# Recommender tower, one core: early chunks in another order, weight preparation between them, gathers issued without waits

## The chip, the core and the metric

The kernel runs on one NeuronCore of a Trainium2 chip. The core has five engines that work in parallel, each through its own instructions in order: TensorE (PE, matrix products; its weight loads are shown as PEld), VectorE (DVE), ScalarE (ACT), GpSimd (POOL) and SyncE (SP, which here only issues DMA transfers). Engines are held together by semaphores: an instruction waits until a counter has reached a value. The metric is the device time of one execution in microseconds. SBUF is the working memory on the core, PSUM the memory that TensorE writes.

## What is computed

A recommendation tower for 512 samples. 26 rows of 64 numbers are gathered for each sample from 26 tables (13,312 rows in all); they are projected, normalised over 128 features, mixed to 32 rows for each sample, normalised over these 32, and multiplied pairwise with each other and with a normalised dense row. The 528 products go through a linear layer and a norm, and then through a small network with the dense inputs beside them:

```python
x = layer_norm(dense_t @ Wd.T, gd, bd)
y = layer_norm(jnp.einsum('bnd,ed->bne', sparse_t, Ws), gs, bs)
y = jnp.einsum('bne,pn->bep', y, Wsi)
y = layer_norm(y, gsi, bsi)
y = jnp.swapaxes(y, 1, 2)
T = jnp.concatenate([x[:, None, :], y], axis=1)
Z = jnp.einsum('bnd,bmd->bnm', T, T)
Zflat = Z[:, TRIL_I, TRIL_J]
out = layer_norm(Zflat @ Wl.T, gl, bl)
...
h = jnp.concatenate([z, r_dense_t], axis=1)
h = jnp.maximum(h @ W_top1 + b_top1, 0.0)
h = jnp.maximum(h @ W_top2 + b_top2, 0.0)
y = h @ W_top3
```

Of the linear layer's 512 columns the network uses the first 384. All arithmetic is in float32.

## The kernel before

The 512 samples are cut into 4 groups of 128 (`NG`), and each group into 4 chunks of 32 (`NC`); chunk n is chunk n % 4 of group n // 4, and there are 16. In the texts c stands for n % 4. POOL gathers the embedding rows with 104 indirect DMAs (L332), 26 for a group, in batches of 8, 6, 6 and 6 for its chunks. The waits ahead of them (`steps`, from chunk 2 on) tie each gather of chunk n to a step of VectorE or TensorE in chunk n - 2; the memory that a gather writes is used by it alone, so no data hangs on these waits.

A chunk n passes through these steps, each a function of the engine's program:

- `transpose_rows` (PE, L1039) turns its gathered rows, ACT copies them from PSUM (`gt_copy`, L424), and `gram_rows` (PE, L1045) multiplies them by a Gram matrix, from which VectorE gets the first variance (`variance1`, L748 and L752). ACT takes its root (`deviation1`, L429) and VectorE scales the rows (`scale_rows`, L766).
- `project_fields` (PE, L1057) mixes the 26 rows to 32, ACT copies the result (`ut_copy`, L433: the projected rows' copy), and `embed` (PE, L1070) applies the projection.
- `y_evacuate` (DVE, L780) adds a bias and writes the chunk into V; `square2` (ACT, L438), `variance2` (DVE, L787), `deviation2` (ACT, L442: the second root) and `normalise2` (DVE, L794 and L796) are the second norm.
- `pair_products` (PE, L1077) forms the products, `z_evacuate` (ACT, L448 to L450) and `z_merge` (DVE, L838) take them to SBUF.

A group, once its four chunks are merged, goes through `spread_pairs` (PE, L1165), `z_copy` (ACT, L499), `project_pairs` (PE, L1119, five blocks of 128), `f_squares` and `deviation3` (ACT), `root3` (DVE), `f_scale` (ACT), `transpose_features` (PE), `zn_copy` (ACT) and `layer1`, `layer2`, `layer3` (PE, L1135, L1145, L1153) with their copies.

The order of the work is written out by hand: each engine runs a function `slot(n)`, for n = 3 to 14 (2 to 14 on VectorE), between a written-out beginning and a written-out end. A slot mixes steps of chunks n, n - 1, n - 2 and n - 3 with steps of the group before. PE's slot is: transpose n, project n - 1, Gram of n, embed n - 1, pair products of n - 2, with one piece of group work in each slot.

Weights are prepared on the chip as well, once: `prepare_b1` (PE, L1001) multiplies 12 blocks of the first layer's weights by a single column each, which is 24 passes of TensorE; `prepare_dense` (L1019) forms the dense inputs' share of the first layer in four parts, two of which are copied and get their bias later (`dense_bias`, L386); `prepare_last_block` (L1029) is five products into one bank, after which ACT works on the result; `prepare_means` and `prepare_gains` scale the weights `wl` of the linear layer on ACT.

## Time and profile before

| | before |
|---|---|
| median of 3 runs | 171.74 us (171.62 to 173.03) |
| profiled execution, its own time | 172.89 us |
| span of the profiled execution | 171.1 us |
| PE busy | 148.5 us (87%) |
| DVE busy | 126.1 us (74%) |
| POOL busy | 100.6 us (59%) |
| ACT busy | 83.5 us (49%) |
| mean granted clock of TensorE | 0.99 |

The profile is one execution. Busy time of an engine is the time in which it has an instruction under way; "idle before" is the time in which it had none ahead of an instruction, and the engine or line behind the arrow is what ended this wait. The span runs from the first to the last instruction, and the execution's own time is 1.8 us more. Times below are in microseconds from the start of the span. The x of a TensorE row counts passes: a float32 product is two of them.

### The profile page before, as it was taken

The page shows a single profiled execution, that of the slowest core. Times are in us where ns is not written, and L with a number is a line of the kernel's source. Part 1 is how long each engine was busy: PE and PEld are TensorE (multiplying, and loading weights), DVE is VectorE, ACT ScalarE, POOL GpSimd, SP SyncE. Part 2 cuts the span into 40 slices and gives each one's busy share as a digit, 9 for nine tenths or more (in the row PEclk, how much of TensorE's full clock was granted, in tenths as well). Part 3 has the DMA queues.
Part 4 walks back from the last instruction along what each step waited for, and adds up shares of the span by engine and source line. Part 5 has one row for each costly group of instructions (what it writes and reads, how often), then busy time and mean ns, then how long its engine had stood idle before and what let it go on. Part 6 is the DMA issues. An engine that isn't in the chain of part 4 may idle for free.

```text
span 171.1 us, 3531 instructions
## 1 busy us (share of the span) xinstructions
PE 148.5 (87%) x1382; PEld 106.7 (62%) x1382; DVE 126.1 (74%) x264; ACT 83.5 (49%) x224; POOL 100.6 (59%) x109
## 2 busy tenths in 40 slices
PE   0489889987977597999999899999998999899995
PEld 0224457937545455646978475678776665689994
DVE  6593755899917795876789988586998997993153
ACT  3011322429677739686546365563438363653250
POOL 1777777777777777777776777777777400040000
PEclk9999999699999999999999999999999999999999
DMA  4913542615111111111111111111111100000000
GB/s 98 338 24 73 190 136 41 201 42 146 26 31 25 33 23 31 27 23 34 24 23 27 31 23 36 24 26 31 23 33 27 23 0 4 0 4 0 4 0 0
DMA packets 5728, 8.14 MB, mean 48 GB/s; under 512 B 2357, under 2 KB 3279, under 8 KB 5712
## 3 DMA queue, kind: packets, MB, share of 16 engines
q0 software_dynamic: 3328, 3.41, 10.8%
q1 hardware_dynamic: 1664, 3.65, 6.9%
q10 hardware_dynamic: 720, 0.85, 1.5%
q8 instruction: 11, 0.18, 0.5%
q14 instruction: 5, 0.04, 0.1%
HBM read 7.91 MB, written 0.00 MB: 46 GB/s over the span
## 4 chain that ended last, share of the span: by engine, by line
PE 60%; DVE 18%; ACT 13%; issue 4%; DMA 3%; SPq 1%; DVEq 0%
PE ps_tail L1119 8%; PE ps_y L1070 6%; PE ps_gq L1045 5%; PE ps_tail L1135 5%; PE ps_ut L1057 5%; PE ps_z L1077 4%; DVE V L796 4%; DVE V L780 4%; PE ps_z L1165 3%; DMA smask<-in_span_mask_dram 3%; PE ps_tail L1029 3%; DVE var L752 3%; ACT sq L438 2%; ACT gt L424 2%; DVE qg L748 2%
## 5 line engine op out<-in xcount | busy, mean ns | idle before, releaser
L332 POOL DMA_INDIRECT G<-in_table_dram,idx x104 | 98.5, 947 | 35.7 <-issue 30.2
L1057 PE MATMUL ps_ut<-S,G 128*128 128x192 f32 (+4 forms) x128 | 21.9, 316 | 2.8 <-DVE G L766 2.8
L1057 PEld LDWEIGHTS ps_ut<-S,G 128*128 128x128 f32 x128 | 20.1, 199 | 4.7 <-DVE G L766 3.4
L780 DVE TENSOR_TENSOR V<-ps_y,bias_y 128x512 f32<-128x512 f32 x32 | 20.5, 683 | 0.8 <-PE ps_y L1070 0.7
L1045 PE MATMUL ps_gq<-gram,gt 128*128 128x128 f32 x104 | 15.6, 289 | 5.9 <-ACT gt L424 5.7
L438 ACT ACTIVATE sq<-V 128x1024 f32<-128x1024 f32 x14 | 14.9, 1061 | 10.6 <-DVE V L780 10.6
L1077 PEld LDWEIGHTS ps_z<-V 128*64 128x64 f32 x448 | 14.3, 136 | 9.2 <-DVE V L796 5.6
L787 DVE TENSOR_REDUCE var<-sq 128x32 f32<-128x1024 f32 x14 | 17.1, 1220 | 3.8 <-ACT sq L438 3.6
L1070 PE MATMUL ps_y<-ut,wcg 64*128 64x512 f32 x64 | 18.1, 639 | 1.8 <-issue 1.7
L1045 PEld LDWEIGHTS ps_gq<-gram,gt 128*128 128x128 f32 x104 | 13.3, 197 | 7.5 <-ACT gt L424 6.4
L1077 PE MATMUL ps_z<-V 128*64 128x67 f32 x448 | 16.2, 224 | 0.1
L429 ACT ACTIVATE sd<-var,eps 128x6 f32<-128x6 f32 (+1 forms) x16 | 4.8, 299 | 20.6 <-DVE var L752 20.6
L748 DVE TENSOR_TENSOR qg<-ps_gq,G 128x384 f32<-128x384 f32 (+1 forms) x16 | 9.4, 586 | 6.6 <-PE ps_gq L1045 6.6
L796 DVE TENSOR_TENSOR V<-V,ps_z 128x1024 f32<-128x1024 f32 x10 | 12.2, 1220 | 0.3
L1119 PE MATMUL ps_tail<-wl,zb 128*128 128x512 f32 x24 | 11.4, 610 | 0.0
L433 ACT COPY ut<-ps_ut 128x512 f32<-128x512 f32 x16 | 9.3, 583 | 4.1 <-PE ps_ut L1057 3.8
L838 DVE COPY_PREDICATED zt<-mmask,ps_z 128x128 f32<-128x128 int32 x28 | 7.1, 313 | 5.0 <-ACT zt L450 5.0
L338 POOL TENSOR_TENSOR V<-V,r_pool 128x1024 f32<-128x1024 f32 x1 | 1.9, 1918 | 14.9 <-DVE r_pool L802 14.9
L424 ACT COPY gt<-ps_gq 128x384 f32<-128x384 f32 (+1 forms) x16 | 8.1, 508 | 4.7 <-PE ps_gq L1039 4.7
L752 DVE TENSOR_REDUCE var<-qg 128x6 f32<-128x384 f32 (+1 forms) x16 | 9.4, 586 | 0.6
L1135 PE MATMUL ps_tail<-zn,w1z 128*128 128x128 f32 x72 | 8.8, 279 | 0.7 <-ACT zn L479 0.7
L766 DVE TENSOR_TENSOR G<-G,ps_y 128x384 f32<-128x384 f32 (+1 forms) x15 | 8.8, 589 | 0.5
(179 smaller groups left out, 237.9 us busy)
## 6 DMA issues: line engine op xcount, KB each, us to landing
G<-in_table_dram,idx POOLq DMA_INDIRECT x104, 2.5
w1z<-in_w_z_dram SPq DMA_DIRECT2D x1, 768.0 KB, 4.3
wl<-in_wl_blocks_dram SPq DMA_DIRECT2D x1, 768.0 KB, 5.8
dns<-in_dense_t_dram ACTq DMA_DIRECT2D x1, 512.0 KB, 4.9
w1d<-in_w_d_dram SPq DMA_DIRECT2D x1, 512.0 KB, 5.3
wl<-in_wl_blocks_dram SPq DMA_DIRECT2D x1, 512.0 KB, 3.5
w2s<-in_w_dram SPq DMA_DIRECT2D x1, 512.0 KB, 3.5
wrow<-in_wsi_rows_dram SPq DMA_DIRECT2D x1, 208.0 KB
```

The lines of the kernel that those rows point to most:

```text
L332: pool.indirect_dma_start(G[:, n // NC, j, g, :], None, table, bass.IndirectOffsetOnAxis(ap=idx[:, k:k + 1], axis=0)).then_inc(gathered[n ...
L438: act.activation(sq2[:, :, :].rearrange("p (b l) q -> p b l q", l=2), chunk_v(n), ACT.Square).then_inc(sq_ready, 1)
L752: dve.reduce_sum(var1[:, 0:2 * count], qg[:, 0:count * P].rearrange("p (t d) -> p t d", d=D), AX_X).then_inc(var1_ready, 1)
L780: dve.tensor_tensor(chunk_v(n)[:, g * CB // 2:(g + 1) * CB // 2, :, :], ps_y[:, g, :].rearrange("p (b l q) -> p b l q", l=2, q=NPROJ), bia ...
L787: dve.reduce_sum(var2[:, :], sq2[:, :, :], AX_X).then_inc(var2_ready, 1)
L796: dve.tensor_tensor(chunk_v(n), chunk_v(n), r2_at(n).rearrange("p (b l) -> p b l", l=2).unsqueeze(3).broadcast_to([P, CB, 2, NPROJ]), ALU. ...
L1045: mm = pe.matmul(ps_gq[:, i * P:(i + 1) * P], gt[:, i * P:(i + 1) * P], gram[:, :], start=True, stop=True)
L1057: mm = pe.matmul(ps_ut[:, chunk % 2, col:col + width], G[:, gp, j, :, :].rearrange("p g d -> p (g d)"), S[:, j, :, :].rearrange("p s q -> ...
L1070: pe.matmul(ps_y[:, g, :], wcg[64 * g:64 * g + 64, :], ut[64 * g:64 * g + 64, :], start=True, stop=True).then_inc(y_ps, 1)
L1077: mm = pe.matmul(z_bank(n)[64 * ct:64 * ct + 64, w, s * SLOTS:(s + 1) * SLOTS], V[:, v, 3:SLOTS], V[:, v, :], start=True, stop=True)
L1119: mm = pe.matmul(ps_tail[:, :], zb[:, k, at] if k < PB else zx[:, at], wl[:, k, :], start=(k == 0), stop=(k == KB - 1))
L1135: mm = pe.matmul(tail[:, oc, :], w1z[:, k, oc * P:(oc + 1) * P], zn[:, k, :], start=(k == 0), stop=(k == LLIVE - 1))
```

## The change

1. **Loads.** SP issues the load of the first layer's weights `w1z` (768 KB) as soon as the dense inputs have landed, and then `w1d` (512 KB); before, `w1d` went first, with no wait, and `w1z` after the first chunk's gathers. Both parts of `wl` are issued after the gathers of chunk 0; before, after those of chunks 1 and 2.
2. **Gathers.** POOL issues all 104 without waits.
3. **Beginning.** PE runs the dense projection ahead of the bias product, then `prepare_b1`, then chunk 0. VectorE adds the bias (`prepare_b1`) before the first variance, and forms x after `scale_rows(0)`. The parts of `prepare_dense` get their bias in the same ACT instruction that takes them from PSUM, so the three `dense_bias` instructions are gone.
4. **Chunks 1 to 3** run in `early_slot`: transposes, products, projection and embedding of chunk n in the same slot, and pair products of n - 2 between transposes and Gram product. `prepare_dense(1)`, `prepare_xsum` and the five products of `prepare_last_block`, cut into 3 and 2, stand between the Gram product and the projection. Slots 4 and 5 are written out, with the spread of group 0 in slot 4 and `project_pairs(0)` in slot 5 (before: both in slot 6).
5. **Later slots.** In slots with c = 1 (9 and 13), `pair_products(n - 2)` stands ahead of `embed(n - 1)` and `spread_pairs` comes at the end of this slot, with `z_copy` on ACT; before, they were in the next slot. VectorE's `z_merge(n - 2)` goes ahead of `variance2(n - 1)`, and ACT's `z_evacuate(n - 2)` ahead of `relu2`. In slots with c = 2, ACT takes the second root ahead of the projected rows' copy.

```diff
+            sp.dma_start(w1z[:, :, :], w1_z).then_inc(ld_w1z, 16)
             sp.dma_start(w1d[:, :, :], w1_d).then_inc(ld_w1d, 16)
-
-            sp.wait_ge(gathered[0][0], 2 * len(batch(0)) * 16)
-            sp.dma_start(w1z[:, :, :], w1_z).then_inc(ld_w1z, 16)
             sp.dma_start(pmask[:, :], pair_mask).then_inc(ld_pm, 16)
             sp.dma_start(mmask[:, :], merge_mask).then_inc(ld_pm, 16)
+            sp.wait_ge(gathered[0][0], 2 * len(batch(0)) * 16)
             for h, (k, end) in enumerate(((0, 2), (2, KB))):
-                sp.wait_ge(gathered[0][1 + h], 2 * len(batch(1 + h)) * 16)
                 sp.dma_start(wl[:, k:end, :], wl_blocks[:, k:end, :]).then_inc(ld_wl[h], 16)
             sp.wait_ge(gathered[0][3], 2 * len(batch(3)) * 16)
             sp.dma_start(w2s[:, :, :], w2).then_inc(ld_w2, 16)
...
-                        if n >= LEAD:
-                            done, value = steps(n - LEAD, 2 * len(js))[2 * (j - js[0]) + g]
-                            if value > 0:
-                                pool.wait_ge(done, value)
...
+            def dense_direct(oc):
+
+                act.wait_ge(b1_ready, 1)
                 act.wait_ge(dense_ps, DENSE_ORDER.index(oc) + 1)
-                act.copy(h1_dense[:, oc, :], dense_banks[oc % 2]).then_inc(dense_sb, 1)
...
+            def early_slot(n):
+
+                gt_copy(n)
+                square2(n - 1)
+                if n == 1:
+                    prepare_means(0)
+                else:
+                    z_evacuate(n - 2)
+                deviation1(n)
+                if n == 1:
+                    dense_direct(1)
+                    prepare_xsum()
+                if n == 2:
+                    prepare_means(1)
+                if n == 3:
+                    prepare_last_block()
+                deviation2(n - 1)
+                ut_copy(n)
+                if n == 3:
+                    prepare_gains((0, 1))
+
             def slot(n):
                 gp, c = divmod(n, NC)
                 if c != 2:
                     z_evacuate(n - 3)
                 if c > 2:
                     deviation2(n - 2)
-                if c == 3 and gp > 0:
+                if c == 3:
                     f_squares(gp - 1)
                     deviation3(gp - 1)
                 gt_copy(n)
-                if c < 2:
...
                     deviation2(n - 2)
                 ut_copy(n - 1)
-                if c == 2:
-                    deviation2(n - 2)
                 if c == 0 and gp > 1:
                     relu1(gp - 2)
-                if c == 2 and gp > 0:
-                    z_copy(gp - 1)
-                if c == 3 and gp > 0:
+                if c == 3:
                     f_scale(gp - 1)
...
                 deviation1(n)
-                if c == 1 and gp > 1:
+                if c == 1:
+                    z_evacuate(n - 2)
                     relu2(gp - 2)
-                if c == 3 and gp > 0:
+                if c == 3:
                     zn_copy(gp - 1)
...
                 if c == 1:
-                    z_evacuate(n - 2)
-                if c == 1 and gp > 1:
                     y_copy(gp - 2)
...
+                    z_copy(gp - 1)
...
             prepare_embedding()
             prepare_x()
-            dense_copy(0)
-            dense_copy(1)
             gt_copy(0)
             deviation1(0)
-            dense_copy(3)
-
-            gt_copy(1)
+            dense_direct(0)
             ut_copy(0)
-            deviation1(1)
-            square2(0)
-
-            gt_copy(2)
-            deviation2(0)
-            ut_copy(1)
-            deviation1(2)
-            square2(1)
-            prepare_xsum()
-            for n in range(3, NCHUNK - 1):
+            for n in range(1, NC):
+                early_slot(n)
+
+            square2(3)
+            gt_copy(4)
+            z_evacuate(2)
...
+            deviation2(3)
+            prepare_gains((2, 3))
+            deviation1(4)
+            z_evacuate(3)
+            dense_direct(2)
+            prepare_gains((4,))
+
+            z_copy(0)
+            dense_direct(3)
+            gt_copy(5)
+            ut_copy(4)
+            deviation1(5)
+            square2(4)
+            for n in range(6, NCHUNK - 1):
...
 
+                dve.wait_ge(ld_sm, 16)
                 dve.wait_ge(b1_ps, 1)
...
+            def early_slot(n):
+
+                variance1(n)
+                if n > 1:
+                    z_merge(n - 2)
+                scale_rows(n)
+                variance2(n - 1)
+                if n == 3:
+                    prepare_shift()
+                normalise2(n - 1)
+                y_evacuate(n)
+                x_slots(n)
+
             def slot(n):
                 gp, c = divmod(n, NC)
-                if n >= 3 and c != 2:
+                if c != 2:
                     z_merge(n - 3)
                 normalise2(n - 2)
-                if c == 3 and gp > 0:
+                if c == 3:
                     root3(gp - 1)
                 if c == 0 and gp > 1:
                     add_dense(gp - 2)
@@ -908,11 +909,9 @@
                 y_evacuate(n - 1)
                 scale_rows(n)
                 x_slots(n - 1)
-                variance2(n - 1)
                 if c == 1:
                     z_merge(n - 2)
-                if n == 3:
-                    prepare_shift()
+                variance2(n - 1)
 
...
-            prepare_x()
+            prepare_b1()
             variance1(0)
             scale_rows(0)
+            prepare_x()
             dve.wait_ge(x_ready, 1)
             x_slots(0)
-
-            variance1(1)
-            dve.wait_ge(bias_ready, 1)
+            prepare_last_block()
             y_evacuate(0)
-            scale_rows(1)
-            variance2(0)
-            prepare_b1()
-            prepare_last_block()
-            for n in range(2, NCHUNK - 1):
+            for n in range(1, NC):
+                early_slot(n)
+
+            variance2(3)
+            z_merge(2)
+            normalise2(3)
+            variance1(4)
+            scale_rows(4)
+            z_merge(3)
+
+            variance1(5)
+            y_evacuate(4)
+            scale_rows(5)
+            x_slots(4)
+            variance2(4)
+            for n in range(6, NCHUNK - 1):
...
+                pe.wait_ge(dense_sb, 1)
...
                 pe.wait_ge(ld_w1d, 16)
-                if oc == 3:
-                    pe.wait_ge(dense_sb, 2)
+                if oc == 0:
+                    pe.wait_ge(b1_ready, 1)
                 elif oc == 2:
-
                     pe.wait_ge(last_ready, 1)
+                elif oc == 3:
+                    pe.wait_ge(dense_sb, 3)
                 for k in range(2):
-                    mm = pe.matmul(dense_banks[oc % 2], w1d[:, k, oc * P:(oc + 1) * P], dns[:, k, :], start=(k == 0), stop=(k == 1))
+                    mm = pe.matmul(dense_banks[oc], w1d[:, k, oc * P:(oc + 1) * P], dns[:, k, :], start=(k == 0), stop=(k == 1))
...
+                    if gp == 0 and k % 2 == 0:
+
+                        pe.wait_ge(wl_ready, k // 2 + 1)
                     mm = pe.matmul(ps_tail[:, :], zb[:, k, at] if k < PB else zx[:, at], wl[:, k, :],
                                    start=(k == 0), stop=(k == KB - 1))
...
+            def early_slot(n):
+
+                transpose_rows(n)
+                if n > 1:
+                    pair_products(n - 2)
+                gram_rows(n)
+                if n == 1:
+                    prepare_dense(1)
+                    prepare_xsum()
+                if n == 2:
+                    prepare_last_block(range(0, 3))
+                if n == 3:
+                    prepare_last_block(range(3, KB))
+                project_fields(n)
+                embed(n)
+
             def slot(n):
                 gp, c = divmod(n, NC)
                 transpose_rows(n)
                 project_fields(n - 1)
                 gram_rows(n)
-                if c == 2 and gp > 0:
-                    spread_pairs(gp - 1)
+                if c == 1:
+                    pair_products(n - 2)
                 embed(n - 1)
-                if c == 3 and gp > 0:
+                if c == 3:
                     transpose_features(gp - 1)
-                pair_products(n - 2)
+                if c != 1:
+                    pair_products(n - 2)
                 if c == 0 and gp > 1:
                     layer2(gp - 2)
-                if c == 1 and gp > 1:
+                if c == 1:
                     layer3(gp - 2)
-                if c == 2 and 0 < gp < NG - 1:
+                    spread_pairs(gp - 1)
+                if c == 2 and 1 < gp < NG - 1:
                     project_pairs(gp - 1)
-                if c == 3 and gp > 0:
+                if c == 3:
                     layer1(gp - 1)
-                if n == 3:
-                    prepare_last_block()
-                if n == 5:
-                    prepare_dense(2)
 
             prepare_embedding()
             prepare_x()
-            prepare_dense(0)
-            prepare_dense(1)
+            prepare_b1()
             pe.wait_ge(patterns_ready, 1)
             transpose_rows(0)
             pe.wait_ge(gram_ready, 1)
             gram_rows(0)
-            prepare_dense(3)
-
-            transpose_rows(1)
-            pe.wait_ge(patterns_ready, 1)
+            prepare_dense(0)
             project_fields(0)
-            gram_rows(1)
             pe.wait_ge(bias_ready, 1)
             pe.wait_ge(x_ready, 1)
             pe.wait_ge(wcg_ready, 1)
             embed(0)
-            prepare_b1()
-
-            transpose_rows(2)
-            project_fields(1)
-            gram_rows(2)
-            embed(1)
-            prepare_xsum()
-            pair_products(0)
-            for n in range(3, NCHUNK - 1):
+            for n in range(1, NC):
+                early_slot(n)
+
+            transpose_rows(4)
+            pair_products(2)
+            gram_rows(4)
+            prepare_dense(2)
+            pair_products(3)
+            spread_pairs(0)
+            prepare_dense(3)
+
+            transpose_rows(5)
+            project_fields(4)
+            gram_rows(5)
+            embed(4)
+            project_pairs(0)
+            for n in range(6, NCHUNK - 1):
                 slot(n)
 
```

How it moves instructions on TensorE at the beginning, up to the first `embed`. Before (L1019 is `prepare_dense`, L1039 and L1045 chunk 0's and 1's transposes and Gram products, L1057 the projection):

```order
L988 MATMUL ps_y<-dns,wd 128x512 x2
L992 MATMUL ps_z<-x_sq,ones 128x512
L1019 MATMUL ps_tail<-dns,w1d 128x512 x2
L1019 MATMUL ps_z<-dns,w1d 128x512 x2
L1039 MATMUL ps_gq<-eye,G 128x128 x4
L1045 MATMUL ps_gq<-gram,gt 128x128 x4
L1019 MATMUL ps_z<-dns,w1d 128x512 x2
L1039 MATMUL ps_gq<-eye,G 128x128 x3
L1057 MATMUL ps_ut<-S,G 128x160
L1057 MATMUL ps_ut<-S,G 128x192 x2
L1057 MATMUL ps_ut<-S,G 128x64
L1057 MATMUL ps_ut<-S,G 128x128
```

and now (L1012 is `prepare_b1`, L1031 `prepare_dense`, L1052, L1058, L1070 and L1083 the steps of chunk 0):

```order
L999 MATMUL ps_y<-dns,wd 128x512 x2
L992 MATMUL ps_y<-wsis,bsr 128x32
L1004 MATMUL ps_z<-x_sq,ones 128x512
L1012 MATMUL ps_tail<-sm,w1z 128x1 x12
L1052 MATMUL ps_gq<-eye,G 128x128 x4
L1058 MATMUL ps_gq<-gram,gt 128x128 x4
L1031 MATMUL ps_tail<-dns,w1d 128x512 x2
L1070 MATMUL ps_ut<-S,G 128x160
L1070 MATMUL ps_ut<-S,G 128x192 x2
L1070 MATMUL ps_ut<-S,G 128x64
L1070 MATMUL ps_ut<-S,G 128x128
L1083 MATMUL ps_y<-ut,wcg 128x512 x2
```

The 12 single-column products stood behind the first `embed`, and stand ahead of chunk 0's transposes; chunk 1 no longer begins before chunk 0 is embedded.

TensorE in slot 9, from chunk 9's Gram products to the start of slot 10. Before (L1070 embeds chunk 8, L1077 is the pair products of chunk 7, L1153 layer 3 of group 0, L1039 the transposes of chunk 10):

```order
L1045 MATMUL ps_gq<-gram,gt 128x128 x3
L1070 MATMUL ps_y<-ut,wcg 128x512 x2
L1077 MATMUL ps_z<-V 64x67 x16
L1153 MATMUL ps_tail<-h,sm 1x128 x2
L1039 MATMUL ps_gq<-eye,G 128x128 x3
```

and now (L1090 pair products of chunk 7, L1083 embed of chunk 8, L1168 layer 3, L1180 `spread_pairs(1)`, L1052 transposes of chunk 10):

```order
L1058 MATMUL ps_gq<-gram,gt 128x128 x3
L1090 MATMUL ps_z<-V 64x67 x16
L1083 MATMUL ps_y<-ut,wcg 128x512 x2
L1168 MATMUL ps_tail<-h,sm 1x128 x2
L1180 MATMUL ps_z<-zt,eye 32x4x32 x8
L1180 MATMUL ps_z<-zt,eye 32x32 x4
L1180 MATMUL ps_z<-zt,eye 32x4x32 x8
L1180 MATMUL ps_z<-zt,eye 32x32 x4
L1052 MATMUL ps_gq<-eye,G 128x128 x3
```

The embedding and the pair products have changed places, and the spread has come ahead of chunk 10's transposes; it stood behind chunk 10's Gram products.

ScalarE at the same place, from `deviation1(9)` to `ut_copy(9)`. Before (L448 to L450 `z_evacuate(7)`, L424 `gt_copy(10)`, L433 `ut_copy(9)`, L442 `deviation2(8)`, L499 `z_copy(1)`):

```order
L429 ACTIVATE sd<-var,eps 128x6
L488 ACTIVATE h<-ps_tail,sm 128x128 x2
L438 ACTIVATE sq<-V 128x1024
L448 COPY zt<-ps_z 128x8x16 x2
L449 COPY zt<-ps_z 128x16
L450 COPY zt<-ps_z 128x16
L493 COPY y_row<-ps_tail 1x128
L424 COPY gt<-ps_gq 128x384
L433 COPY ut<-ps_ut 128x512
L442 ACTIVATE sd<-var,eps 128x32
L499 COPY zb<-ps_z 128x2x4x64
```

and now (L430 to L432, L481 and L482 `z_copy(1)`, L406 `gt_copy(10)`, L424 `deviation2(8)`, L415 `ut_copy(9)`):

```order
L411 ACTIVATE sd<-var,eps 128x6
L430 COPY zt<-ps_z 128x8x16 x2
L431 COPY zt<-ps_z 128x16
L432 COPY zt<-ps_z 128x16
L470 ACTIVATE h<-ps_tail,sm 128x128 x2
L420 ACTIVATE sq<-V 128x1024
L475 COPY y_row<-ps_tail 1x128
L481 COPY zb<-ps_z 128x2x4x64
L482 COPY zx<-ps_z 64x128
L406 COPY gt<-ps_gq 128x384
L424 ACTIVATE sd<-var,eps 128x32
L415 COPY ut<-ps_ut 128x512
```

`z_copy(1)`, which waits for the spread, was behind `deviation2(8)`, and is now ahead of `gt_copy(10)` and of it.

## Rows read from the trace of the kernel before

**Rows 1.** Page of the profile, part 1: busy time, share, instructions of TensorE.
```profile
PE 148.5 (87%) x1382; PEld 106.7 (62%) x1382; DVE 126.1 (74%) x264; ACT 83.5 (49%) x224; POOL 100.6 (59%) x109
```

**Rows 2.** Timeline of TensorE, beginning: start, us, line, op, operands, passes, idle before.
```profile
8.47 3.78 PE L988 MATMUL ps_y<-dns,wd 128*128 128x512 f32 x4
...
27.44 1.13 PE L1070 MATMUL ps_y<-ut,wcg 64*128 64x512 f32 x4
28.50 2.84 PE L1001 MATMUL ps_tail<-sm,w1z 128*128 128x1 f32 x24
```

**Rows 3.** Windows: length, busy by engine, granted clock, DMA share, GB/s.
```profile
30.00:31.00 1.00, 1.00 (x11) 1.00 (x11) 0.59 (x2) 1.00 (x1) 0.70 (x2) 1.00 0.13 25
...
33.00:34.00 1.00, 1.00 (x7) 1.00 (x6) 0.96 (x7) 0.00 (x0) 0.80 (x1) 0.50 0.89 348
```

**Rows 4.** Timeline of TensorE: transposes of chunks 7, 8 and 14.
```profile
76.90 0.49 PE L1039 MATMUL ps_gq<-eye,G 128*128 128x128 f32 x3
...
84.80 0.60 PE L1039 MATMUL ps_gq<-eye,G 128*128 128x128 f32 x4
...
129.79 0.55 PE L1039 MATMUL ps_gq<-eye,G 128*128 128x128 f32 x3
```

**Rows 5.** Page, part 5: groups; busy, mean ns of one, idle before.
```profile
L780 DVE TENSOR_TENSOR V<-ps_y,bias_y 128x512 f32<-128x512 f32 x32 | 20.5, 683 | 0.8 <-PE ps_y L1070 0.7
L438 ACT ACTIVATE sq<-V 128x1024 f32<-128x1024 f32 x14 | 14.9, 1061 | 10.6 <-DVE V L780 10.6
L787 DVE TENSOR_REDUCE var<-sq 128x32 f32<-128x1024 f32 x14 | 17.1, 1220 | 3.8 <-ACT sq L438 3.6
L748 DVE TENSOR_TENSOR qg<-ps_gq,G 128x384 f32<-128x384 f32 (+1 forms) x16 | 9.4, 586 | 6.6 <-PE ps_gq L1045 6.6
L766 DVE TENSOR_TENSOR G<-G,ps_y 128x384 f32<-128x384 f32 (+1 forms) x15 | 8.8, 589 | 0.5
```

**Rows 6.** The chain of waits: start, us, what; slots 6 and 7.
```profile
72.57 4.50 PE ps_tail L1119 x10
77.10 0.70 ACT f_sq L467 x2
77.82 0.29 ACT sd L471
78.11 0.37 ACT gt L424
```

**Rows 7.** Timeline of TensorE, slots 9 and 10.
```profile
94.23 1.13 PE L1070 MATMUL ps_y<-ut,wcg 64*128 64x512 f32 x4
95.42 1.16 PE L1077 MATMUL ps_z<-V 128*64 128x67 f32 x32
...
100.58 1.41 PE L1165 MATMUL ps_z<-zt,eye 64*32 64x128 f32 x48
102.29 1.13 PE L1070 MATMUL ps_y<-ut,wcg 64*128 64x512 f32 x4 [0.30 <-issue]
```

**Rows 8.** Timelines of VectorE (first row) and of ScalarE, the same stretch.
```profile
96.33 1.28 DVE L780 TENSOR_TENSOR V<-ps_y,bias_y 128x512 f32<-128x512 f32 x2
...
100.21 0.32 ACT L442 ACTIVATE sd<-var,eps 128x32 f32<-128x32 f32 x1
102.04 0.59 ACT L499 COPY zb<-ps_z 128x512 f32<-128x512 f32 x1 [1.50 <-PE ps_z L1165]
```

**Rows 9.** Timeline of GpSimd: three of the 104 gathers.
```profile
20.12 1.20 POOL L332 DMA_INDIRECT G<-in_table_dram,idx  x1 [0.30 <-issue]
...
91.28 0.94 POOL L332 DMA_INDIRECT G<-in_table_dram,idx  x1 [0.93 <-DVE V L780]
...
126.21 0.94 POOL L332 DMA_INDIRECT G<-in_table_dram,idx  x1 [0.30 <-issue]
```

**Rows 10.** Page, part 6: issues; count, KB each, us to landing.
```profile
G<-in_table_dram,idx POOLq DMA_INDIRECT x104, 2.5
w1z<-in_w_z_dram SPq DMA_DIRECT2D x1, 768.0 KB, 4.3
```

65 lines of the change are left out of this document (19 added, 46 removed).

## The prediction

> **What bounds the kernel now.** I read the page's busy shares first, then the clock over stretches, then the chain of waits and the timelines of PE, VectorE, ScalarE and GpSimd side by side. PE is busy for 148.5 of 171.1 us [rows 1], so at most 22.6 us are to be had from its waits, and some 4 us of these are the start, before it has anything to do. From chunk 8 on it is nearly closed. What decides there is a cycle through two engines: VectorE works without a pause from the start of a group to the middle of slot 9, then PE does, through the spread, an embedding, pair products, ten passes of `project_pairs` and layer 1. GpSimd hands out a gather every 1.25 us, and its last chunk-14 gather starts at 126.21 and lands some 2.5 us later, while the transposes of chunk 14 begin at 129.79 [rows 4, 9, 10]. So the gathers are close behind the work without bounding it: about 1.1 us of slack at chunk 14.
>
> The sum is made against the profiled execution (172.89 us, span 171.1). The difference is then set on the median of the runs, 171.74, which is 0.6 above the span. A measurement of this kernel can't tell less than about 1% from nothing.
>
> **Start: 1.1 us gained (bounds: 3.0 gained, 2.6 lost).** The dense projection began at 8.47 behind the bias product [rows 2]; VectorE has its weights about 1.5 us sooner, so I let it begin at 7.1. Its two products took 3.8, then the x square, a product of 2.1 and a root: x's root is formed by about 17.7, and PE is free at 13.4. The load of `w1z` issued at about 7.1 lands 4.3 later [rows 10], in time. Now come the 24 passes of `prepare_b1`, which took 2.84 us [rows 2] at 28.5, mostly at a granted clock of 1.00 (2.4 GHz). But just after them, at 33, the granted clock was 0.50 (1.2 GHz), although PE had been busy all through 30 to 31 [rows 3]. And early in the kernel PE was slow too: the four passes at 8.47 took 3.78, where ten passes of this width took 4.50 at 72.57 [rows 2, 6], so the first ones ran at about half the pace. I therefore price `prepare_b1` as slow work at a slow time, between 2.84 and 5.7 us, and take 5 (nearest to the slow rows around it). Then chunk 0: transposes from about 18.4, copy, Gram product, a variance of two instructions (1.2 to 1.4), root, scaling 0.9, projection 1.6, copy 0.6. That puts `embed(0)` at 26.3, against 27.44 [rows 2]. With all of it at the fast clock it would be 24.4; with all at the slow one 30. In return the dip at 33 goes, since `prepare_b1` is no longer there: that is inside the next step, which uses fast prices.
>
> **From embed(0) to chunk 8's transposes: 4.0 lost (bounds: 2.5 to 5.5).** Before it took 84.80 - 27.44 = 57.4 us [rows 2, 4]. Now I count from an embedding's start, e. A slot of the new order is a closed loop, because chunk n is not begun before n - 1 is embedded: PE goes on at e + 1.1, transposes, does 1.1 of pair products, waits for nothing, and has the Gram product out at e + 3.5; variance 1.2; the merge 0.4; root and scaling 0.8 (to e + 5.9); `variance2` of n - 1 takes 1.2, its root 0.3, and only then does ScalarE reach `ut_copy`, 0.6: the next embedding starts at e + 8.0 [rows 5]. PE's own work in it is 6.5 to 7.3 us, so the weight preparation does fill most of the waits, but the loop through VectorE is longer than it. Slots 1 and 2 come to 8.0 each. Slot 3 comes to 8.4, since `prepare_last_block` on ScalarE (2.1) now stands ahead of the second root. Slots 4 and 5: `gt_copy(4)` stands behind `square2(3)` (PE waits 1.4), and the spread of group 0 waits for the last merge, which stands behind variance and scaling of chunk 4 (PE waits 1.9). With 12 us of PE work besides, `embed(4)` starts 15.8 after `embed(3)`, and `project_pairs(0)` (1.1, then 4.5 [rows 6]) ends 5.6 later. Slot 6 is 5.0: chunk 7's transposes are at embed(0) + 50.7, that is 77.0 by my start, where they were at 76.90 [rows 4].
>
> Slot 7 then gives up more. Before, `project_pairs(0)` stood in slot 6 and VectorE used that time to catch up; its 7.9 us were PE work without a gap. Now VectorE's `variance2(5)` ends 2.5 after chunk 7's transposes begin, and on ScalarE its root, `f_squares` 0.7, `deviation3` 0.3 and `gt_copy(7)` 0.4 follow it in order [rows 6], ahead of PE's Gram product. Slot 7 takes 10.7. Sum: 8.0 + 8.0 + 8.4 + 15.8 + 5.6 + 5.0 + 10.7 = 61.5, less the 0.1 by which the first slot is shorter: 61.4.
>
> **Slots 9 and 13: 2.5 lost in each, 5.0 (bounds 1.2 to 2.7 each).** This is the step that I trust most. The pair products of chunk 7 start at 95.42, as soon as VectorE has normalised it; the embedding of chunk 8 started at 94.23 [rows 7]. With their places changed it starts at 95.42 + 1.09 = 96.5. Its first half is usable 1.13 later, at 97.6, and `y_evacuate(8)` ran from 96.33 [rows 7, 8], with no pause before it: VectorE, which has no slack here, loses 1.2. Next, `z_merge(7)` now stands ahead of `variance2(8)`: 0.4. The spread waits for this merge and can start at 100.1; PE has layer 3 behind it and nothing else, and idles 1.7. `z_copy(1)` follows the start of a spread by 102.04 - 100.58 = 1.46 and takes 0.85 [rows 7, 8], so ScalarE is held to 102.4, with `gt_copy(10)` and `deviation2(8)` queued behind. The second root ran at 100.21 [rows 8]; now it is at 102.8. The embedding of chunk 9, which waits for the normalisation that follows this root, goes from 102.29 [rows 7] to 104.8, and the rest of the group hangs on it. That the root has been put ahead of `ut_copy` gives back 0.5 at most and is counted in this. Slot 13 has the same neighbours. The written-out end of the kernel stays as it was and moves as a whole.
>
> **At no cost.** The three `dense_bias` instructions that go (0.7 each) stood where ScalarE waits anyway. Gathers without waits: one wait of 0.93 instead of the usual 0.30 [rows 9] was the longest, 1.0 us by chunk 14; the work is later than that by far, so nothing comes of it. `wl` now loads in one stretch after chunk 0's gathers and is there long before its use in slot 1 to 3.
>
> Sum: -1.1 + 4.0 + 5.0 = +7.9, which makes **179.6 us** (172.89 + 7.9 = 180.8 for an execution like the profiled one).
>
> **Rivals.**
>
> - *The clock is fast from the start (179.6 - 1.9 = 177.7).* PE's first work is closer together now, and if the clock has risen before `prepare_b1`, chunk 0 is embedded at 24.4. For it: the first product begins 1.4 sooner. Against: the slow rows and the 0.50 behind `prepare_b1` [rows 2, 3]. Chance 0.20.
> - *The clock stays slow to the embedding of chunk 0 (179.6 + 3.7 = 183.3 at the most, about 182.5).* Chance 0.08.
> - *The swap in slots 9 and 13 costs nothing (179.6 - 5.0 = 174.6).* So it would be if the chain through VectorE had slack that I don't see, for instance if it has run ahead by more than 2.5 us by slot 8. Against: in the old order it pauses at the start of slot 8 for a root, which brings it back in step. Chance 0.13.
> - *No change (171.7).* Early gain and late loss cancel, at 5 each. Chance 0.10.
> - *Faster.* The early slots' waits are what the weight preparation fills: if the loop of 8.0 falls to PE's own 6.5 to 7.3 and the waits in slots 4 and 7 go, chunk 7 is 5 us ahead or more, and this more than pays slots 9 and 13. Then the gathers decide. They are free of their waits, so chunk 14 could begin 1.0 + 0.9 = 1.9 sooner than 129.79 and no more [rows 4, 9, 10]: 169.8. It turns to this side where slots 1 to 7 gain more than 5 us. For it: PE's 22.6 us of waits [rows 1]; against: every loop above goes through VectorE. Chance 0.12.
>
> To the last there is a point on the gathers. One took 1.20 us, at 20.12, while VectorE ran a `tensor_scalar` from SBUF to SBUF; the others took 0.94 [rows 9]. The Trainium skill (SBUF — State Buffer, "Who interferes with whom") says that such an instruction takes a port pair for its whole length and that GpSimd, generating descriptors, "fully blocks". The row agrees in kind (0.26 more). By that rule gathers that are no longer tied to VectorE's steps would be hit more often, and if each of the 14 small copies after it (0.2 each) hit one, the last case would be 2.8 us worse and no longer faster; the forecast, which isn't bound by gathers, would not change.
>
> The forecast has 0.37. Slower by over 1%: 0.37 + 0.20 + 0.08 + 0.13 = 0.78; within 1%: 0.10; faster by over 1%: 0.12. Left out of the range are the faster case and what lies above 183: 171.5 to 183. The forecast's own range is 177 to 182.
>
> **What would show it.** In the new profile: `prepare_b1` at 13.4, longer than 2.84 us; the first `embed` near 26; then embeddings 8.0, 8.0 and 8.4 apart, with PE idle ahead of projections and waiting on `ut`; chunk 7's transposes near 77, chunk 8's near 88, with the Gram product of chunk 7 held by `gt_copy` behind `f_squares`; in slots 9 and 13 PE idle ahead of the spread, VectorE idle ahead of `y_evacuate`, and 34.4 us from one group to the next where it was 31.9. I am wrong if VectorE turns out to have slack in slot 8, if the early slots come to less than 7.5 us, or if the gathers are what PE waits for.

## The result, and the profile after

| | before | changed |
|---|---|---|
| median | 171.68 us (170.64 to 173.03, 4 executions) | 181.36 us (179.89 to 185.32, 4 executions) |
| ratio to before | | 1.046 [1.039, 1.053] |
| profiled execution, its own time | 172.89 us | 179.96 us |
| its span | 171.1 us | 178.1 us |
| mean granted clock | 0.99 | 0.96 |

The changed kernel is slower. The ratio leaves out its two longest executions (182.75 and 185.32) as disturbed. The forecast was 179.6 for the median, and 180.8 for an execution like the profiled one, whose time is 179.96. The profiled spans differ by 7.0 us, and the profile's page says first that TensorE's work has hardly grown: 1.3 us more busy time than in [rows 1]. The rest is waiting.

Page of the changed kernel, parts 1 and 2 (the clock in 40 slices) and groups of part 5:

```profile
PE 149.8 (84%) x1382; PEld 108.3 (61%) x1382; DVE 126.4 (71%) x264; ACT 82.2 (46%) x221; POOL 100.5 (56%) x109
PEclk9995699999999999999999969999998799999999
L320 POOL DMA_INDIRECT G<-in_table_dram,idx x104 | 98.4, 946 | 34.6 <-issue 31.4
L769 DVE TENSOR_TENSOR V<-ps_y,bias_y 128x512 f32<-128x512 f32 x32 | 20.5, 683 | 3.1 <-PE ps_y L1083 3.0
```

VectorE had 0.8 us of idle time ahead of `y_evacuate` [rows 5]; now it has 3.1. The gathers take what they took, and nothing waits for them. The clock fell in three places.

Timeline of TensorE in the changed kernel, its beginning and the start of the early slots:

```profile
6.91 3.75 PE L999 MATMUL ps_y<-dns,wd 128*128 128x512 f32 x4 [1.08 <-DMA dns<-in_dense_t_dram]
...
11.35 1.12 PE L1004 MATMUL ps_z<-x_sq,ones 128*128 128x512 f32 x2 [0.35 <-ACT x_sq L353]
12.31 3.56 PE L1012 MATMUL ps_tail<-sm,w1z 128*128 128x1 f32 x24
15.73 1.09 PE L1052 MATMUL ps_gq<-eye,G 128*128 128x128 f32 x4
...
24.85 1.13 PE L1083 MATMUL ps_y<-ut,wcg 64*128 64x512 f32 x4 [0.77 <-ACT ut L415]
```

Windows of the same kernel (length, busy time of five engines, granted clock, DMA share, GB/s):

```profile
12.00:14.00 2.00, 2.00 (x18) 1.76 (x17) 1.23 (x2) 0.69 (x1) 1.39 (x3) 1.00 0.40 97
14.00:16.00 2.00, 2.00 (x12) 2.00 (x12) 2.00 (x2) 0.00 (x0) 1.70 (x2) 0.50 0.30 41
```

The x square's sum took 1.12 us, about half of what TensorE needs for two such passes when it is slow (2.07, below), so the engine had come up to speed by 11; the clock fell from 2.4 to 1.2 GHz during the one-column products of `prepare_b1` (1.00 in the window before 14, 0.50 in the one behind it) and was back at 21. `embed(0)` starts at 24.85, 2.6 sooner than in [rows 2]. Not all of this is the change's: in the profiled execution of the kernel before the square's sum took 2.07 us, so that one came up to speed later. How much is left when like is compared with like stands under e4.

The embeddings of chunks 1 to 3 follow at 32.86, 40.80 and 49.22, that of chunk 4 at 64.82. Slot 7 and chunk 8's transposes, and slots 9 and 10, timeline of TensorE:

```profile
75.40 0.55 PE L1052 MATMUL ps_gq<-eye,G 128*128 128x128 f32 x3
76.42 1.31 PE L1070 MATMUL ps_ut<-S,G 128*128 128x192 f32 x8 [0.47 <-DVE G L755]
79.69 0.94 PE L1058 MATMUL ps_gq<-gram,gt 128*128 128x128 f32 x6 [1.97 <-ACT gt L406]
...
85.96 0.60 PE L1052 MATMUL ps_gq<-eye,G 128*128 128x128 f32 x4
...
96.57 1.16 PE L1090 MATMUL ps_z<-V 128*64 128x67 f32 x32 [1.21 <-DVE V L785]
97.66 1.13 PE L1083 MATMUL ps_y<-ut,wcg 64*128 64x512 f32 x4
...
101.38 1.41 PE L1180 MATMUL ps_z<-zt,eye 64*32 64x128 f32 x48 [1.82 <-DVE zt L827]
102.72 0.90 PE L1052 MATMUL ps_gq<-eye,G 128*128 128x128 f32 x3
103.41 2.29 PE L1070 MATMUL ps_ut<-S,G 128*128 128x192 f32 x8
...
106.61 1.13 PE L1083 MATMUL ps_y<-ut,wcg 64*128 64x512 f32 x4
```

And the other engines there, VectorE (first three rows) and ScalarE, from the same kernel's timelines:

```profile
98.82 1.29 DVE L769 TENSOR_TENSOR V<-ps_y,bias_y 128x512 f32<-128x512 f32 x2 [1.25 <-PE ps_y L1083]
...
101.23 1.22 DVE L776 TENSOR_REDUCE var<-sq 128x32 f32<-128x1024 f32 x1
104.46 0.36 DVE L783 RECIPROCAL ps_y<-sd 128x32 f32<-128x32 f32 x1 [2.00 <-ACT sd L424]
...
102.84 0.58 ACT L481 COPY zb<-ps_z 128x512 f32<-128x512 f32 x1 [1.50 <-PE ps_z L1180]
103.44 0.26 ACT L482 COPY zx<-ps_z 64x128 f32<-64x128 f32 x1
103.73 0.48 ACT L406 COPY gt<-ps_gq 128x384 f32<-128x384 f32 x1
104.10 0.32 ACT L424 ACTIVATE sd<-var,eps 128x32 f32<-128x32 f32 x1
```

To be read in this order: VectorE stands still for 1.25 us because the embedding of chunk 8 now waits behind the pair products, which themselves wait 1.21 for the normalisation of chunk 7; the spread waits 1.82 for the merge, which VectorE does only behind its evacuation of chunk 8; ScalarE waits for the spread in `z_copy` and only then takes the second root, 1.65 after its input was there (101.23 + 1.22 to 104.10); VectorE waits 2.00 for that root; and `embed(9)` starts 20.65 after chunk 8's transposes, where it was 102.29 - 84.80 = 17.49 [rows 4, 7].

The whole difference then lies in three stretches: chunk 8's transposes at 85.96 instead of 84.80, +1.16; from there to `embed(9)` 20.65 instead of 17.49, +3.16; and the rest, in slot 13 and behind it, 7.0 - 1.16 - 3.16 = +2.7 (chunk 12's transposes to chunk 15's take 25.07, and took 22.32).

### The profile page after: what moved, and what is told of

Its sections match the earlier page's. It is cut to its first block, busy times and chain, and to the rows that moved or that the text cites. A ratio compares the mean times of both kernels' runs of the same rounds, so it can differ in the third digit from the quotient of the medians.

```text
span 178.1 us, 3530 instructions
## 1 busy us (share of the span) xinstructions
PE 149.8 (84%) x1382; PEld 108.3 (61%) x1382; DVE 126.4 (71%) x264; ACT 82.2 (46%) x221; POOL 100.5 (56%) x109
## 4 chain that ended last, share of the span: by engine, by line
PE 58%; DVE 23%; ACT 11%; issue 4%; DMA 3%; ACTq 1%; DVEq 0%
PE ps_y L1083 8%; PE ps_tail L1134 8%; PE ps_z L1090 6%; PE ps_gq L1058 5%; PE ps_tail L1150 5%; PE ps_ut L1070 5%; DVE V L769 4%; DVE var L776 4%; PE ps_z L1180 3%; PE ps_gq L1052 3%; ACT sq L420 3%; DVE V L785 3%; DMA dns<-in_dense_t_dram 3%; PE ps_y L999 2%; PE ps_tail L1012 2%
## 5 line engine op out<-in xcount | busy, mean ns | idle before, releaser
L1070 PEld LDWEIGHTS ps_ut<-S,G 128*128 128x128 f32 x128 | 21.1, 207 | 6.6 <-DVE G L755 6.3
L1070 PE MATMUL ps_ut<-S,G 128*128 128x192 f32 (+4 forms) x128 | 22.8, 326 | 2.1 <-DVE G L755 2.0
L1083 PE MATMUL ps_y<-ut,wcg 64*128 64x512 f32 x64 | 18.1, 640 | 4.2 <-ACT ut L415 3.5
L1058 PE MATMUL ps_gq<-gram,gt 128*128 128x128 f32 x104 | 16.3, 299 | 4.7 <-ACT gt L406 4.6
L1090 PEld LDWEIGHTS ps_z<-V 128*64 128x64 f32 x448 | 14.3, 136 | 8.4 <-DVE V L785 5.1
L1090 PE MATMUL ps_z<-V 128*64 128x67 f32 x448 | 16.2, 224 | 2.4 <-DVE V L785 2.4
L1058 PEld LDWEIGHTS ps_gq<-gram,gt 128*128 128x128 f32 x104 | 14.1, 207 | 5.8 <-ACT gt L406 4.5
L406 ACT COPY gt<-ps_gq 128x384 f32<-128x384 f32 (+1 forms) x16 | 8.1, 505 | 15.6 <-PE ps_gq L1052 15.5
L785 DVE TENSOR_TENSOR V<-V,ps_z 128x1024 f32<-128x1024 f32 x11 | 13.4, 1221 | 0.4
L415 ACT COPY ut<-ps_ut 128x512 f32<-128x512 f32 x16 | 9.3, 583 | 5.6 <-PE ps_ut L1070 5.3
L1180 PE MATMUL ps_z<-zt,eye 64*32 64x128 f32 (+1 forms) x192 | 5.7, 346 | 5.5 <-DVE zt L827 5.5
L1052 PEld LDWEIGHTS ps_gq<-eye,G 128*128 128x128 f32 x52 | 6.8, 159 | 5.4 <-issue 5.1
L1052 PE MATMUL ps_gq<-eye,G 128*128 128x128 f32 x52 | 9.9, 310 | 0.0
```

The source lines that it names most:

```text
L785: dve.tensor_tensor(chunk_v(n), chunk_v(n), r2_at(n).rearrange("p (b l) -> p b l", l=2).unsqueeze(3).broadcast_to([P, CB, 2, NPROJ]), ALU. ...
L1052: mm = pe.transpose(ps_gq[:, i * P:(i + 1) * P], G[:, gp, j + i, :, :].rearrange("p g d -> p (g d)"), eye[:, :])
L1058: mm = pe.matmul(ps_gq[:, i * P:(i + 1) * P], gt[:, i * P:(i + 1) * P], gram[:, :], start=True, stop=True)
L1070: mm = pe.matmul(ps_ut[:, chunk % 2, col:col + width], G[:, gp, j, :, :].rearrange("p g d -> p (g d)"), S[:, j, :, :].rearrange("p s q -> ...
L1083: pe.matmul(ps_y[:, g, :], wcg[64 * g:64 * g + 64, :], ut[64 * g:64 * g + 64, :], start=True, stop=True).then_inc(y_ps, 1)
L1090: mm = pe.matmul(z_bank(n)[64 * ct:64 * ct + 64, w, s * SLOTS:(s + 1) * SLOTS], V[:, v, 3:SLOTS], V[:, v, :], start=True, stop=True)
```

## The experiments

For each kernel three marks of its profile are compared: where `embed(0)` starts, the stretch from there to chunk 8's transposes (the early part), and the stretch from these to the end (the late part). Slot 7 is counted from chunk 7's transposes to chunk 8's. Each row is one profiled execution, and only executions with the same course of the clock can be compared to the tenth. In the variants of the changed kernel (e9 apart) an early part that differs from 61.1 by more than slot 7 does comes from a fall of the clock: in e3 and e10 at 48 and in e1 and e6 at 61 to 63 the stretch from `embed(3)` to `embed(4)` took 16.4 to 17.3 us instead of 15.6, and in e11 that from `embed(2)` to `embed(3)` took 9.6 instead of 8.4. In e4 falls at 28 and at 52 make up the 1.0 over the kernel before. The medians were measured in groups, and the kernel before, run beside each, had 171.68 (changed), 172.66 (e1 to e4), 172.65 (e5 to e8), 172.26 (e9, e10) and 171.68 in one execution (e11, e12).

| kernel | median | span | embed(0) | early part | of it slot 7 | late part |
|---|---|---|---|---|---|---|
| before | 171.68 | 171.1 | 27.4 | 57.4 | 7.9 | 86.3 |
| changed | 181.36 | 178.1 | 24.9 | 61.1 | 10.6 | 92.1 |
| e1, slots 9, 10, 13, 14 as before | 181.11 | 179.1 | 27.6 | 65.6 | 13.5 | 85.9 |
| e2, embedding first again | 179.54 | 177.9 | 25.1 | 63.8 | 13.4 | 89.0 |
| e3, spread in its old place | 181.34 | 177.6 | 24.3 | 64.8 | 13.5 | 88.5 |
| e4, before with new slots 9, 10, 13, 14 | 177.55 | 175.7 | 25.2 | 58.4 | 7.9 | 92.1 |
| e5, projection in slot 6 | 180.03 | 178.3 | 24.8 | 61.3 | 7.9 | 92.2 |
| e6, e1 and e5 together | 175.24 | 174.2 | 25.5 | 62.9 | 7.9 | 85.8 |
| e7, 8 of 24 passes of `prepare_b1` | 180.65 | 179.2 | 24.4 | 62.6 | 12.1 | 92.2 |
| e8, before without gather waits | 172.13 | 170.9 | 27.3 | 57.4 | 7.9 | 86.2 |
| e9, e6 with a shorter early loop | 177.48 | 173.8 | 25.6 | 62.4 | 7.9 | 85.8 |
| e10, filled wait in slots 9, 13 | 182.59 | 178.2 | 24.5 | 62.0 | 10.6 | 91.7 |
| e11, one product of `prepare_last_block` | 185.45 (one execution) | 183.6 | 27.4 | 64.0 | 12.1 | 92.2 |
| e12, short `variance2` in slots 1 to 3 | 183.57 (one execution) | 181.7 | 27.5 | 62.5 | 12.1 | 91.7 |

**e1, the later slots as before.** In TensorE's `slot` of the changed kernel (VectorE's merge, ScalarE's `z_evacuate` and `z_copy` went back with it):

```diff
+                if c == 2 and gp > 1:
+                    spread_pairs(gp - 1)
+                embed(n - 1)
                 if c == 1:
                     pair_products(n - 2)
-                embed(n - 1)
...
-                    spread_pairs(gp - 1)
```

> The changed kernel with the later slots' order put back (embedding ahead of pair products, spread and its copy in the next slot, the merge behind the second variance). Theory A (these queue orders cost 3.2 and 2.8 us in slots 9 and 13, by the spans from chunk 8 to 12 and 12 to 15): span 5.5 to 6 shorter than 178.1, near 172.3, and chunk 12's transposes 31.9 after chunk 8's. Rival B (the early order leaves the engines in another step, which is what slots 9 and 13 suffer from): less than 2 us are won.

Measured: 181.11 us (175.58 to 181.64). The late part is 85.9, that of before within 0.4, so the order of these slots is worth 6.2 us in the profile. The time is not 6 us shorter, though: in the profiled execution `embed(0)` came 2.8 later, slot 4 took 1.7 more and slot 7 2.9 more, and all three are TensorE at half pace (below). With these the spans add up: -6.2 + 2.8 + 1.7 + 2.9 = +1.2, and 179.1 - 178.1 is 1.0. The step from chunk 8's transposes to chunk 12's is 31.76, as theory A had it; its span of 172.3 did not come. The fastest execution had a span of 173.8.

**e2 and e3, one half each.** e2 puts `embed(n - 1)` ahead of the pair products again and leaves the spread in slots 9 and 13; e3 puts spread, `z_copy` and merge back and leaves the pair products first.

The edit of e2:

```diff
+                embed(n - 1)
                 if c == 1:
                     pair_products(n - 2)
-                embed(n - 1)
```

> The changed kernel with only the embedding back ahead of the pair products in slots 9 and 13. Theory A: VectorE's idle 1.2 ahead of y_evacuate(8) goes, the merge and the spread come 1.2 sooner, but z_copy still holds ScalarE: 1.2 to 1.4 won in each slot, span near 175.5, or 174.5 if the slow clock behind the spread goes with it. Rival C (only the spread's place costs anything): nothing won.

> The changed kernel with spread, its copy and the merge back in their old places, pair products still ahead of the embedding. Theory A: TensorE's 1.8 ahead of the spread goes and ScalarE isn't held, but VectorE still waits 1.2 for the embedding; embedding 9 starts some 18.2 to 18.7 after chunk 8's transposes (17.5 in the kernel before, 20.65 now): about 2 to 2.4 won in each slot, span near 173.7. Rival C: all of it is won, 5.9, span near 172.2.

Measured: e2 179.54 us, 1.034 [1.023, 1.045] of before; e3 181.34. Late parts of 89.0 and 88.5, against 92.1 with both and 85.9 with neither: the new place of the spread (with its merge and copy) costs 3.1 by itself, the pair products' place 2.6, and together they cost 6.2, of which 0.4 is a fall of the clock that neither half had (e10, below). Neither half is free: that only the spread's place costs is refuted. Against theory A, e2 wins 3.1 where 2.4 to 2.8 stood, with that 0.4 in it, and e3 wins 3.6, less than the 4 to 4.8 that A had, although its `embed(9)` comes 18.61 after chunk 8's transposes, as A put it. e2's profile also shows what raised the early part. Timeline of TensorE in e2, slot 7:

```profile
79.81 1.65 PE L1058 MATMUL ps_gq<-gram,gt 128*128 128x128 f32 x6 [1.97 <-ACT gt L406]
81.39 2.08 PE L1083 MATMUL ps_y<-ut,wcg 64*128 64x512 f32 x4
...
86.13 2.94 PE L1150 MATMUL ps_tail<-zn,w1z 128*128 128x128 f32 x24
```

and its windows:

```profile
78.00:80.00 2.00, 0.19 (x1) 0.19 (x2) 1.97 (x5) 1.80 (x6) 1.43 (x2) 0.79 0.12 27
80.00:82.00 2.00, 2.00 (x8) 1.67 (x10) 0.72 (x3) 0.82 (x2) 1.66 (x2) 0.50 0.21 41
```

The same instructions wait as long (1.97) as in the changed kernel, and then take twice as long (2.08 for 1.13): the wait ahead was followed by a fall of the clock in this execution, and not in the other.

**e4, only the new slots.** The kernel before with the order of slots 9, 10, 13 and 14 of the changed one.

```diff
+                if c == 1 and gp > 1:
+                    pair_products(n - 2)
                 embed(n - 1)
...
+                    spread_pairs(gp - 1)
```

> The kernel before with the new order in slots 9, 10, 13 and 14 alone. Theory A: 5.0 to 5.9 lost against the kernel before, span near 176.6, with embedding 9 at 20 to 20.7 after chunk 8's transposes. Rival B: under 2 us lost.

Measured: 177.55 us, 1.027 [1.019, 1.035]; late part 92.1, to 0.1 us that of the changed kernel. So these slots cost 5.8 us in the trace (92.1 - 86.3) and 4.9 in the median (against 172.66) whatever stands ahead of them.

This trace shows something else too. Its beginning is that of the kernel before, instruction for instruction, and yet `embed(0)` starts at 25.20. Timeline of TensorE in the kernel before (first row) and in e4:

```profile
12.93 2.07 PE L992 MATMUL ps_z<-x_sq,ones 128*128 128x512 f32 x2 [0.69 <-ACT x_sq L362]
...
12.35 1.12 PE L996 MATMUL ps_z<-x_sq,ones 128*128 128x512 f32 x2 [0.69 <-ACT x_sq L362]
...
25.20 1.13 PE L1074 MATMUL ps_y<-ut,wcg 64*128 64x512 f32 x4
```

So both beginnings have an early and a late kind. With the early rise `embed(0)` is at 25.20 in the old order (e4) and at 24.85 in the changed kernel (24.3 to 25.6 in its six variants of that kind); with the late rise it is at 27.44 and 27.34 in the old order (before, e8) and at 27.37 to 27.63 in the new one (e11, e12, e1). Compared kind by kind, the new beginning gains 0.35 us or nothing, and most of the 2.6 is the difference between two executions. (The comparison of the late kinds is rough: in the old order the pace has risen by 18, in the new one between 22 and 25, and there are only two and three executions.) One reason for this can be read in the same rows: in the new order the fall of the clock behind the one-column products comes at 14, so that chunk 0's Gram product takes 2.05 us (1.13 in e4).

**e5, the projection alone.**

```diff
-                if c == 2 and 1 < gp < NG - 1:
+                if c == 2 and 0 < gp < NG - 1:
...
             embed(4)
-            project_pairs(0)
```

> The changed kernel with project_pairs(0) alone moved back from behind embed(4) to slot 6. In the changed kernel's trace embed(0) to chunk 8's transposes takes 61.1 us (57.4 before), with slot 7 at 10.6 us and a granted clock of 0.50 in slot 7 in some executions. Theory A (the projection stands in a slot that TensorE already fills, and slot 7 then has 3.3 us of idle TensorE that it could cover): the stretch shrinks by 2 to 3 us to 58 to 59, the clock stays at 1.00 in slot 7, chunk 8's transposes start near 83.5 and the span is near 175.5. Rival B (the chunks of slots 5 to 7 are held by the chain through VectorE and ScalarE, 8 us each, wherever the projection stands): the stretch stays within 0.7 us of 61.1 and the span near 178.

Measured: 180.03 us (179.71 to 182.62), early part 61.3. Rival B holds. Slot 7 falls to 7.9 as in the kernel before, and slot 6, apart from the projection's own 4.4 us, gives all of it back: TensorE waited 0.72 + 0.47 + 1.97 = 3.2 us from `embed(5)` to the Gram product of chunk 7, and now waits 1.59 + 1.67 = 3.3 us in slot 6, both times for VectorE (the profile names nothing for the second wait, but it ends at 71.66, with VectorE's normalisation of chunk 4 done at 71.55, and `embed(5)` waits for that). Timeline of TensorE in e5:

```profile
67.95 1.34 PE L1070 MATMUL ps_ut<-S,G 128*128 128x192 f32 x8 [1.59 <-DVE G L755]
69.13 0.86 PE L1058 MATMUL ps_gq<-gram,gt 128*128 128x128 f32 x6
71.66 1.13 PE L1083 MATMUL ps_y<-ut,wcg 64*128 64x512 f32 x4 [1.67 <-issue]
```

**e6, both put back.** e1 and e5 together; the start, the shallower order and the free gathers stay.

> The changed kernel with slots 9, 10, 13, 14 in their old order (as in the first experiment, whose stretch from chunk 8's transposes to the end took 85.9 us against 92.1) and project_pairs(0) back in slot 6. What stays of the change is its start, its embeds one slot earlier, its gathers without waits. Theory A: 25 + 58.5 + 86 = 169.5 us span, 171.3 us time, if the clock stays at 1.00 behind the start. Rival B (the projection's place is worth nothing): 25 + 61.1 + 86 = 172 us span, 174 us time, and 3 us more where the clock falls in slot 7.

Measured: 175.24 us (173.83 to 178.17), 1.011 [1.002, 1.021]. The late part is 85.8; the early one 62.9, of which 1.6 is a `prepare_dense` at half pace at 61 (its four passes took 3.60 there and 1.98 in e5). It is the best version with the new start and still slower than the kernel before, by 0.2 to 2.1%. With the later slots as before and 61.3 for the early part at the fast clock, where the kernel before has 57.4, the 3.9 us that are left belong to the new order of slots 1 to 5 and the weight preparation in them (its start has no share in this stretch, and the gathers cost nothing, e8); no experiment here takes them away.

**e7, a short `prepare_b1`.**

```diff
-                    for k in range(LLIVE):
+                    for k in range(LLIVE - 1, LLIVE):
...
```

> The changed kernel with prepare_b1 cut from 24 products of one column to 8; it leaves out two thirds of that layer's shift. In the changed kernel they start at 12.31, the granted clock is 0.50 from 14 to about 20.5, and embed(0) starts at 24.85. Theory A (the clock falls because TensorE does little but these one-column products for over 3 us): it stays at 1.00, the products take near 1.0 us, the dense projection behind them 1.9 instead of 2.6, and embed(0) starts near 21.5 to 22. Rival B (the clock falls because of the idle time ahead of them): it still falls near 14, and embed(0) starts at 23 to 24.

Measured: `embed(0)` at 24.43, 0.4 sooner: later than either theory had it, and nearest to B's 23 to 24. The windows show 1.00 from 4 to 28, so the fall at 14 is gone, as A said; but the work didn't become faster. Timeline of TensorE in e7:

```profile
11.34 2.07 PE L1004 MATMUL ps_z<-x_sq,ones 128*128 128x512 f32 x2
13.21 1.71 PE L1012 MATMUL ps_tail<-sm,w1z 128*128 128x1 f32 x8
15.16 1.09 PE L1052 MATMUL ps_gq<-eye,G 128*128 128x128 f32 x4 [0.25 <-DMA G<-in_table_dram,idx]
```

The square's sum took 2.07 us at a recorded 1.00, so this execution is of the late kind, and the eight passes ran at half pace (1.71 us, a third of the 5.12 that 24 take in e12). The experiment doesn't decide between A and B: e1, e11 and e12, with all 24 passes and a late rise, show no fall at 14 either. What it does show is that chunk 0 could not start before 15.16, since its last rows land then: against the changed kernel 16 passes fewer brought the transposes forward by 0.57. Where the rise is early, nearly all of `prepare_b1` stands in a wait; where it is late, chunk 0's transposes come at 18.0 to 18.3, 2.9 or more behind their rows.

**e8, gathers without waits in the kernel before.**

```diff
-                        if n >= LEAD:
...
-                                pool.wait_ge(done, value)
```

> The kernel before with the gathers' waits removed and nothing else. Theory A (GpSimd issues one gather in 1.25 us and is never held by these waits for long): time within 0.5 us of before's 172.7, the mean gather 0.94 to 0.95 us. Rival B (gathers that now run beside VectorE's longest blocks are slowed, or slow it): a mean gather over 1.0 us, and 1 us or more later. Rival C (the waits cost time): 1 us or more faster.

Measured: 172.13 us against 172.65, 0.9985 [0.995, 1.002]; one gather takes 945 ns. Nothing, as in theory A. No slowing beside VectorE can be seen at this size.

**e9, a shorter early loop** (on e6). In TensorE's `early_slot` (the old places of e6 are kept; on ScalarE, `z_evacuate` goes behind `deviation1` and `ut_copy` ahead of the second root; on VectorE the merge goes behind the scaling; in slot 4 the last evacuation and merge of group 0 go first):

```diff
                 transpose_rows(n)
+                gram_rows(n)
                 if n > 1:
                     pair_products(n - 2)
-                gram_rows(n)
```

> The kernel of the last experiment but two (old order in slots 9, 10, 13, 14, projection of group 0 in slot 6) with the loop of the early slots made shorter: the Gram product ahead of the pair products in slots 2 and 3, z_evacuate behind deviation1, the merge behind the scaling, ut_copy ahead of the second root, and in slot 4 the last merge of group 0 ahead of the scaling of chunk 4. Embeddings of chunks 0 to 3 start 7.9 to 8.4 us apart there, and embed(0) to chunk 8's transposes takes 61.1 at the fast clock. Theory A (each chunk waits for a loop through VectorE and ScalarE, and its length is the gap): gaps of 7.2 to 7.6 for chunks 2 and 3, the spread of group 0 0.5 to 1 us sooner, 2 us in all: stretch 59, and 170 us span (171.8 us time) where the clock holds. Rival B (the loop's time is given back in slots 5 to 7, where VectorE catches up): gaps shorter, stretch still 61, 172 us span. Rival C (the gaps are TensorE's own work): nothing moves.

Measured: 177.48 us (174.94 to 177.62), 1.027 [1.020, 1.033] of before, in the median above e6's 175.24. The medians don't settle it: four of the six executions have a span of 175.7 or 175.8, 1.9 more than the profiled one (173.8), and weren't profiled. The profile does. The gaps are 7.8, 8.7 and 8.9: longer in slots 2 and 3, which no theory had. The Gram product has to wait 0.57 for `gt_copy` in any case; the pair products had filled this wait and now came behind it, ahead of the products that precede the projection, which start 4.12 after the embedding's start instead of 3.40. The early part is 62.4, and e6's without its half-paced `prepare_dense` would be 61.3. The changed kernel's place for the pair products was the better one; what the other exchanges of this experiment do by themselves isn't shown.

**e10, the wait ahead of the spread filled** (on the changed kernel).

```diff
             def layer3(gp):
                 pe.wait_ge(h2_ready, gp + 1)
+                if gp < 2:
+                    for i in range(3):
+                        for k in range(OC2):
+                            pe.matmul(tail[:, 0, :], w2s[:, k, 0:P], h2[:, k, :], start=True, stop=True)
```

> The changed kernel with six products of 128 x 128 (12 passes, about 1.7 us, their results overwritten) put ahead of layer 3 in slots 9 and 13, into the 1.8 us in which TensorE waits for the merge of chunk 7 (11). Nothing waits for layer 3's result there. In the changed kernel the granted clock is 0.50 from about 103 to 106 and 137 to 140, and chunk 8's transposes to the end take 92.1 us. Theory A (the clock falls because TensorE has idled just before): it stays at 1.00 in both places, the projection of chunk 9 takes 1.3 us instead of 2.3, and the stretch is 0.7 to 1.5 us shorter, 90.6 to 91.4. Rival B (the clock falls for another reason): 0.50 again in both places and 92.1.

Measured: no fall in either place. Timeline of TensorE in e10, slots 9 and 10:

```profile
99.49 1.60 PE L1170 MATMUL ps_tail<-h,w2s 128*128 128x128 f32 x12 [0.17 <-ACT h L470]
...
101.95 1.41 PE L1184 MATMUL ps_z<-zt,eye 64*32 64x128 f32 x48 [0.33 <-DVE zt L827]
...
103.68 1.23 PE L1070 MATMUL ps_ut<-S,G 128*128 128x192 f32 x8
...
106.75 1.13 PE L1083 MATMUL ps_y<-ut,wcg 64*128 64x512 f32 x4 [0.98 <-issue]
```

The projection takes 1.23 instead of 2.29. But the late part only goes from 92.1 to 91.7, less than the 0.7 to 1.5 that A had: `embed(9)` now waits 0.98, for the normalisation behind the second root, so most of what the fall cost lay in that wait. In slot 13 it cost nothing: from chunk 12's transposes to the end it is 57.0 with and without the fall.

That the wait made the clock fall (A) fits, but this one execution doesn't prove it. With the wait left as it is, both places show a fall in the changed kernel, e4, e5, e7 and e11, and neither does in e12. Timeline of TensorE in e12:

```profile
105.37 1.41 PE L1180 MATMUL ps_z<-zt,eye 64*32 64x128 f32 x48 [1.83 <-DVE zt L827]
...
107.10 1.23 PE L1070 MATMUL ps_ut<-S,G 128*128 128x192 f32 x8
```

So the fall is frequent behind this wait and not certain, and a second execution without it may be chance. Its price is confirmed: e12's late part, with nothing filled, is 91.7 as well.

**e11 and e12, what the early gap of 8 us is made of** (one execution each, on the changed kernel). e11 changes `prepare_last_block`, e12 `variance2`:

```diff
-                for k in ks:
+                for k in [k for k in ks if k == KB - 1]:
...
```
```diff
-                dve.reduce_sum(var2[:, :], sq2[:, :, :], AX_X).then_inc(var2_ready, 1)
+                dve.reduce_sum(var2[:, :], sq2[:, :, 0:(NPROJ // 4 if n < 3 else NPROJ)], AX_X).then_inc(var2_ready, 1)
```

> The changed kernel with one of the five products of prepare_last_block left (it leaves out four fifths of that sum), which takes 2.7 us of TensorE's work out of slot 2 and 1.3 out of slot 3. In the changed kernel embed(1), (2), (3) start 8.01, 7.94 and 8.42 us after the one before. Theory A (the slots' length is the loop over VectorE and ScalarE; the products stand in TensorE's waits): the gaps stay within 0.3 of 8.0, 7.9 and 8.4. Rival B (the gaps are TensorE's own work): the second falls to 6 or so and the third to about 7.2.

> The changed kernel with variance2 of chunks 0 to 2 over a quarter of its input (it leaves out three quarters of those sums), about 0.3 instead of 1.21 us, in slots 1 to 3. Theory A (VectorE's instruction stands ahead of the second root and so of ut_copy and the embedding): each gap shrinks by 0.5 to 0.9, to 7.1 to 7.5 (slot 3: 7.5 to 7.9), and embed(3) starts 1.8 to 2.7 us sooner after embed(0). Rival B (TensorE or ScalarE holds them): the gaps stay within 0.2.

Measured: e11's gaps are 8.0, 8.1 and 9.6, e12's 7.8, 7.9 and 8.4. Timeline of TensorE in e11, slot 2 and the start of slot 3:

```profile
41.54 1.28 PE L1070 MATMUL ps_ut<-S,G 128*128 128x192 f32 x8 [2.59 <-DVE G L755]
43.49 2.08 PE L1083 MATMUL ps_y<-ut,wcg 64*128 64x512 f32 x4 [0.68 <-ACT ut L415]
```

ScalarE in the changed kernel (first two rows) and in e12:

```profile
31.88 0.32 ACT L424 ACTIVATE sd<-var,eps 128x32 f32<-128x32 f32 x1 [0.64 <-DVE var L776]
32.22 0.58 ACT L415 COPY ut<-ps_ut 128x512 f32<-128x512 f32 x1
...
34.64 0.58 ACT L415 COPY ut<-ps_ut 128x512 f32<-128x512 f32 x1 [0.43 <-PE ps_ut L1070]
...
42.58 0.58 ACT L415 COPY ut<-ps_ut 128x512 f32<-128x512 f32 x1 [0.18 <-PE ps_ut L1070]
```

With 2.7 us of TensorE's work gone, TensorE waits 2.59 for the scaled rows, and chunk 2 is embedded no sooner: these products did stand in a wait. (The 9.6 goes with a fall of the clock that followed; the windows show 0.50 from 44 to 46, and the embedding takes 2.08 for 1.13.) With VectorE's second variance down to 0.41 us next to nothing is gained either: A had 0.5 to 0.9 for each slot, and only slot 1 is shorter, by 0.2. The rows say why. In slots 1 and 2 three branches meet at ScalarE's copy of the projected rows, and end within some 0.2 us of each other: VectorE's first variance and scaling, TensorE's own products (both of these through the projection), and VectorE's second variance with the root. In the changed kernel the copy follows the root without a pause; in e12, with the root sooner, it waits 0.43 and 0.18 for the projection. In slot 3 it stands behind ScalarE's part of `prepare_last_block` in both kernels. e11 cut the second branch and e12 the third; the first was cut by neither, and that cutting all three would shorten the gap was not tried.

## Why the prediction was right, and where it was off

| step | forecast | profile |
|---|---|---|
| start, to `embed(0)` | 1.1 gained | 2.6 gained (0 to 0.35 like with like) |
| `embed(0)` to chunk 8's transposes | 4.0 lost (61.4) | 3.75 lost (61.1) |
| slots 9 and 13 | 5.0 lost | 5.8 lost |
| `dense_bias`, gathers, `wl` | 0 | 0 (e8 for the gathers) |
| sum | +7.9 | +7.0 |

- **Slots 9 and 13** were the step trusted most, and they carry the result: e1 takes 6.2 away and e4 brings 5.8, on both kernels. The mechanism is in the rows as put: VectorE idle 1.25 (forecast 1.2), TensorE idle 1.82 ahead of the spread (1.7), the second root behind `z_copy`. `embed(9)` was forecast 2.5 later and came 3.16 later; 0.4 of this is the fall of the clock behind the spread's wait (20.65 against 20.26 in e10 and 20.29 in e12), which the sum had at the fast clock. Of the remaining 0.26, 0.12 lies ahead of the spread and the rest between it and the embedding.
- **The early part** was right in size and almost in each gap: 8.01, 7.94, 8.42 and 15.60 where 8.0, 8.0, 8.4 and 15.8 stood, slot 7 10.56 for 10.7. Two of its reasons were only half right. The gap was put down to `variance2` and the second root ahead of `ut_copy`, with TensorE's own 6.5 to 7.3 us well inside it. That path does close last in slots 1 and 2, but two others end within some 0.2 us of it, so e12 shortens it and the gap stays; and the sign that TensorE would be idle ahead of the projections came in slot 3 only (0.68). That the forecast of 8.0 held doesn't show that its path was the only one. Slot 7's loss was put down to `project_pairs(0)` having left slot 6; e5 puts it back, slot 7 recovers, and slot 6 loses as much. The wait is VectorE's and ScalarE's, and the projection's place only decides in which slot it shows.
- **The start** is the term that was wrong, and that the sum came out near the profile is in part luck. Its 1.1 was worked out against a kernel before with a late rise, and the changed kernel was profiled with an early one: 2.6 gained. Like with like it is 0.35 (e4) or nothing (27.44 against 27.37 to 27.63). In the executions with a late rise, the case that the forecast was made for, its working holds up to chunk 0's transposes: `prepare_b1` at 13.0 to 13.3 (forecast 13.4) took 5.12 (5), and the transposes come at 18.0 to 18.3 (18.4). What it missed is behind them: it had the Gram product and the first part of `prepare_dense` at full pace, they took 2.05 and up to 3.62 at half, and `embed(0)` came at 27.4 to 27.6 for 26.3. In the profiled execution TensorE was free 1.1 sooner than forecast, `prepare_b1` took 3.56, and the way from the transposes to `embed(0)` was 1.2 longer, since the clock had fallen. So the two rivals on the clock are not other cases of the kernel: executions differ, and those of the kernel before do too.
- **With a late rise in both kernels** chunk 8's transposes go from 84.80 to 89.96 (e12), of which 1.6 is the fall in slot 7: +3.6, where start and early part together were forecast at +2.9 and the two profiled executions show +1.2.
- **The median** is 1.8 us above the forecast although the profile is 0.8 below its own (179.96 for 180.8). Of eight profiled executions with `project_pairs(0)` in its new place, six had a slot 7 of 12.1 to 13.5 us, with the clock fallen, and two of 10.6; of the six with it in slot 6, none had more than 7.9. The longer executions of the changed kernel exceed the profiled one by 2.9 and 5.4 in span, with a mean granted clock of 0.953 and 0.935 for its 0.962. The first is the size of a fall in slot 7; the second has more than that, and a late rise would not lower the recorded clock (e12 has 0.991). Which falls they had isn't shown: they weren't profiled. That the start gains nothing like with like would also put the median above the forecast.
- The rivals "no change" and "faster" are out: their gain of 5 us in the early slots needed gaps under 7.5, and none came. That the swap is free is refuted by e1 and e4. Of the rule on VectorE and GpSimd that was cited there (the Trainium skill, SBUF — State Buffer, "Who interferes with whom") no run shows a cost for the kernel: a gather takes 946 ns on average in the changed kernel and 945 in e8. The one gather of 1.20 us on which the point rested has its like in e8, beside the same instruction of VectorE (0.55 us at 19.64): at 20.01, it took 0.99.

## What to carry to other kernels

Filling one engine's waits is worth only what waits for that engine: here the last block's products do run in gaps, and chunks came no sooner, since two paths through other engines were as long. Before two steps are exchanged in a tight pipeline, read which engine has no idle time there, and what stands behind the exchanged steps in the queues of the others: 1.2 us of delay for VectorE and a root behind a copy became 2.9 us for each group. A wait of 1.8 to 2 us on TensorE can be paid for twice, since the work behind it may run at half the clock: 0.4 us in slot 9, nothing in slot 13, 1.6 to 2.9 in slot 7. And before a term is read off two profiles, the same instruction's duration should be compared in both: the start's 2.6 us were mostly two executions of different kinds.

## What the runs showed of the hardware

- **The granted clock fell behind waits of TensorE, and not in each execution.** After 1.97 us without work in slot 7 (and 0.47 shortly before) it was 0.50, 1.2 GHz, in e2 and 1.00 in the changed kernel, with the same instructions. Of six executions with a wait of 1.82 or 1.83 ahead of the spreads of slots 9 and 13, five showed a fall behind both, and e12 behind neither (1.00, 2.4 GHz). With twelve passes in this wait there was none (e10, one execution).
- **It can also fall while TensorE is busy**: during or just behind the 24 passes of one column, at 14 in the changed kernel, at 28 in e4 and between 31 and 32 in the kernel before [rows 3]. Where TensorE was still at half pace from the beginning (e1, e7, e11, e12), the record shows no fall there, with 24 passes or with 8.
- **A recorded clock of 1.00 doesn't mean full speed at the beginning.** In e12 the windows show this from 12 to 16 (and 1.00 up to 82):

```profile
12.00:14.00 2.00, 2.00 (x7) 1.25 (x6) 0.26 (x1) 0.67 (x1) 1.39 (x3) 1.00 0.28 58
14.00:16.00 2.00, 2.00 (x11) 2.00 (x11) 1.96 (x2) 0.01 (x1) 1.66 (x2) 1.00 0.42 55
```

while its timeline of TensorE has half the pace of later passes of the same form (`prepare_dense` took 1.88 for four at 30 us):

```profile
11.21 2.07 PE L1004 MATMUL ps_z<-x_sq,ones 128*128 128x512 f32 x2
13.08 5.12 PE L1012 MATMUL ps_tail<-sm,w1z 128*128 128x1 f32 x24
...
21.76 3.58 PE L1031 MATMUL ps_tail<-dns,w1d 128*128 128x512 f32 x4
```

So for the first 25 us an instruction's own duration is the thing to read. The Trainium skill (TensorE: Matmul & The Clock Gate, "What's actually happening") says of the rise at a kernel's start that its point moves from run to run. The traces agree: the same two passes at 11 took 1.12 us in the changed kernel and 2.07 in e7 and e12. What decides in which execution the pace rises at 11 and in which at 18 (the kernel before, e8) or at 22 to 25 (e7, e1, e11, e12) stays open.
